# Attention, state-space and routed layers on one core: links of two VectorE chains placed apart

## The reference, cut to what matters

```python
def _L0_attn_a_ref(x, norm_w, Wq, bq, Wk, bk, Wv, bv, Wo, bo):
    ...
    scores = jnp.einsum('bhqd,bhkd->bhqk', q, k) * scale
    causal = jnp.triu(jnp.ones((T, T), dtype=bool), k=1)
    scores = jnp.where(causal, jnp.asarray(-jnp.inf, dtype=scores.dtype), scores)
    attn = jax.nn.softmax(scores, axis=-1)
    out = jnp.einsum('bhqk,bhkd->bhqd', attn, v)
    ...
# state-space layer, one step over the 512 tokens, for 16 states
    decay = jnp.exp(A[None] * dt[:, :, None])
    inp = dt[:, :, None] * xt_[:, :, None] * bt[:, None, :]
    h = decay * h + inp
    y = jnp.einsum('bdn,bn->bd', h, ct)
```

## Time and profile before

| | us |
|---|---|
| median of 3 runs | 2156.38 |
| lowest and highest | 2152.31, 2167.72 |
| the profiled execution | 2161.24 |
| its span, first to last instruction | 2159.4 |

### The profile page before, as it was taken

One profiled execution on the slowest core, in us unless ns is written; L12 is line 12 of the kernel. 1 busy time (PEld: TensorE's weight loads), 2 busy tenths in 40 slices (PEclk: granted clock), 3 DMA queues, 4 the chain that ended last, 5 costly groups with the idle time before them and its releaser, 6 DMA issues.

```text
span 2159.4 us, 33647 instructions
## 1 busy us (share of the span) xinstructions
PE 1842.8 (85%) x11409; PEld 1132.2 (52%) x11440; DVE 1684.1 (78%) x2586; ACT 1407.4 (65%) x2724; POOL 1040.1 (48%) x930
## 2 busy tenths in 40 slices
PE   5779888998989798988989898898989898877775
PEld 3446454645556464645556464655656464635333
DVE  5343678889788888879787888879887888987783
ACT  2445767686676767677675867677675767574531
POOL 0000364556555464646555464646555464666430
PEclk8999999999999999999999999999999999999998
DMA  4312377666767576667767686666767676652110
GB/s 115 83 52 59 93 152 153 145 142 150 159 140 159 124 170 140 151 128 154 158 148 157 129 171 130 146 142 149 156 141 157 133 157 135 139 112 61 45 59 10
DMA packets 185916, 275.53 MB, mean 128 GB/s; under 512 B 33537, under 2 KB 125586, under 8 KB 185746
## 3 DMA queue, kind: packets, MB, share of 16 engines
q1 hardware_dynamic: 155506, 163.27, 30.5%
q0 software_dynamic: 30240, 110.11, 27.6%
HBM read 128.58 MB, written 34.08 MB: 75 GB/s over the span
## 4 chain that ended last, share of the span: by engine, by line
PE 44%; ACT 19%; DMA 16%; SPq 7%; issue 6%; DVE 5%; POOL 2%; ACTq 0%; POOLq 0%; DVEq 0%
PE bank L314 7%; DMA sk<-qk_parts 7%; PE bank L518 5%; PE bank L323 5%; SPq L726 5%; ACT dec L910 3%; PE bank L372 3%; ACT pt L795 3%; PE bank L395 3%; PE bank L420 3%; PE bank L501 3%; DMA qk_parts<-parts 3%; DMA out<-X 3%; PE bank L482 3%; PE bank L308 2%
## 5 line engine op out<-in xcount | busy, mean ns | idle before, releaser
L1158 DVE TENSOR_TENSOR_SCAN hc<-dec,inp 128x1024 f32<-128x1024 f32 x256 | 613.1, 2395 | 33.0 <-ACT dec L910 28.6
L1331 POOL TENSOR_TENSOR inp<-u,b_all 128x512 f32<-128x512 f32 x256 | 341.1, 1332 | 421.9 <-DVE hc L1158 177.5
L795 ACT ACTIVATE pt<-bank 128x512 f32<-128x512 f32 x640 | 373.8, 597 | 220.4 <-PE bank L397 217.6
L372 PE MATMUL bank<-sk,sq 96*128 96x512 bf16 (+3 forms) x1024 | 279.6, 312 | 95.4 <-DMA sk<-qk_parts 64.4
L1337 POOL TENSOR_TENSOR inp<-u,b_all 128x512 f32<-128x512 f32 x240 | 350.0, 1458 | 18.8
L910 ACT ACTIVATE dec<-dt,a_neg 128x511 f32<-128x511 f32 x512 | 338.0, 717 | 31.4 <-DVE hc L1158 31.4
L1167 DVE TENSOR_TENSOR hc<-hc,bank 128x1024 f32<-128x1024 f32 x242 | 293.6, 1213 | 50.6 <-PE bank L557 49.9
L395 PE MATMUL bank<-sq,sk 98*128 98x512 bf16 (+3 forms) x1024 | 275.4, 307 | 34.1 <-ACT pt L795 28.1
L1344 POOL DMA_DIRECT2D y<-hc x210 | 185.6, 884 | 244.8 <-DMA y<-hc 122.9
L1026 DVE TENSOR_REDUCE mall<-bank 128x1 f32<-128x512 f32 x256 | 172.6, 674 | 100.3 <-PE bank L374 100.0
L372 PEld LDWEIGHTS bank<-sk,sq 96*128 96x128 bf16 x1024 | 102.3, 100 | 213.9 <-DMA sk<-qk_parts 73.0
(11 more groups left out here) (168 smaller groups left out, 3534.2 us busy)
## 6 DMA issues: line engine op xcount, KB each, us to landing
y<-hc POOLq DMA_DIRECT2D x210, 512.0 KB, 5.5
b_all<-b_kept SPq DMA_DIRECT2D x256, 256.0 KB, 4.0
qk_parts<-parts SPq DMA_DIRECT2D x96, 256.0 KB, 2.5
sq<-qk_parts SPq DMA_DIRECT2D x384, 64.0 KB, 3.6
sk<-qk_parts SPq DMA_DIRECT2D x384, 64.0 KB, 3.8
X<-in_x SPq DMA_DIRECT2D x16, 512.0 KB, 5.9
out<-X SPq DMA_DIRECT2D x16, 512.0 KB, 5.9
sq<-hlt SPq DMA_DIRECT2D x256, 2.0 KB
```

The lines of the kernel that those rows point to most:

```text
L372: mm(dst[:, o:o + n], sq[0:KS, slot, h, qb * P:(qb + 1) * P], sk[0:KS, slot, h, 0:n], start=True, stop=False)
L795: A(pt[:, n % PT, :], score_bank[unit % 2][:, :], ACT.Exp).then_inc(exp_done.sem, 1)
L1158: V.tensor_tensor_scan(h, d, v, 0.0, ALU.mult, ALU.add).then_inc(scan_done.sem, 1)
L1331: first = G.tensor_tensor(inp[:, n % 2, 0, :], u[:, 0, :], b_all[:, k % 3, :], ALU.mult)
```

## The change

The four operations of `finish_maxima` become functions of their own, and so do the two of `head_norm`, each signalling by a semaphore of its own in place of the shared `dve_own`. Their places: join behind the scan of p = 5; high part behind the maximum of p = 6, low part behind the product of p = 6; transpose behind the maximum of p = 7, where all four stood. Reciprocals at p = 4 as before; the multiplication at p = 5, behind the maximum there. What is computed is the same, and so is the number of operations. The other engines' orders don't change.

```diff
--- before.py
+++ after.py
@@ -112,7 +112,7 @@
               "gated": 246, "add_x3": (251, 251), "in1": 265, "out1": 268, "add_up1": (277, 280), "stats_q": -102}
     POOL_AT = {"rsqrt_f": 99, "rsqrt_s": 124, "rsqrt_q": -104, "inputs": 151, "rsqrt_l": 254, "low": (111, 266)}
     SP_AT = {"parts": (-43, -4), "load_x": -119, "store_b": 155, "store": 281}
-    FINISH = 14
+    JOIN_DVE = 5
     HEADS_PE, HEADS_DVE = 4, 4
 
     ctx = ExitStack()
@@ -259,12 +259,16 @@
         m_stacked = tally("max_rows_stacked", TB, 16)
         mx_ready = tally("scores_for_max", UN)
         mx_done = tally("maxima", UN)
+        joined = tally("blocks_joined", 1)
+        high_done = tally("high_parts_of_maxima", 1)
+        low_done = tally("low_parts_of_maxima", 1)
         negm_done = tally("negative_maxima", 1)
         st_ready = tally("scores_ready", UN)
         exp_done = tally("exps", UN)
         pv_done = tally("products_with_values", SETS)
         ot_done = tally("outputs_copied", 1)
         heads_turned = tally("outputs_turned", 1)
+        sums_done = tally("sums_of_exps", 1)
         heads_done = tally("outputs_normalised", 1)
 
         var = [tally(f"variance{k}", 1) for k in range(4)]
@@ -1028,27 +1032,37 @@
                     V.tensor_reduce(mall[:, w, h, 0:4], max_bank[m % 2][:, :].rearrange("p (k n) -> p k n", k=TB),
                                     AXX, ALU.max).then_inc(mx_done.sem, 1)
 
-            def finish_maxima(G):
-
-                w = G % 2
+            def join_blocks(G):
+
                 dve.wait_ge(mx_done.sem, mx_done.at(G))
-                V.tensor_reduce(mall[:, w, :, 5], mall[:, w, :, 0:3], AXX, ALU.max).then_inc(dve_own.sem, 1)
-                dve.wait_ge(dve_own.sem, dve_own.one())
-                four = mall[:, w, :, 3:7]
-                V.tensor_scalar(hl[:, 0, :, :], four, -1.0, None, ALU.mult).then_inc(dve_own.sem, 1)
-                dve.wait_ge(dve_own.sem, dve_own.one())
-                V.scalar_tensor_tensor(hl[:, 1, :, :], four, -1.0, hl[:, 0, :, :], ALU.mult,
-                                       ALU.subtract).then_inc(dve_own.sem, 1)
+                V.tensor_reduce(mall[:, G % 2, :, 5], mall[:, G % 2, :, 0:3], AXX, ALU.max).then_inc(joined.sem, 1)
+
+            def negate_high(G):
+
+                dve.wait_ge(joined.sem, joined.at(G))
+                V.tensor_scalar(hl[:, 0, :, :], mall[:, G % 2, :, 3:7], -1.0, None, ALU.mult).then_inc(high_done.sem, 1)
+
+            def negate_low(G):
+
+                dve.wait_ge(high_done.sem, high_done.at(G))
+                V.scalar_tensor_tensor(hl[:, 1, :, :], mall[:, G % 2, :, 3:7], -1.0, hl[:, 0, :, :], ALU.mult,
+                                       ALU.subtract).then_inc(low_done.sem, 1)
+
+            def turn_maxima(G):
+
                 dve.wait_ge(m_stacked.sem, m_stacked.at(G - 1))
-                dve.wait_ge(dve_own.sem, dve_own.one())
+                dve.wait_ge(low_done.sem, low_done.at(G))
                 V.transpose(hlt[:, :], hl[:, :, :, :].rearrange("p a h q -> p (a h q)")).then_inc(negm_done.sem, 1)
+
+            def head_sums(G):
+                dve.wait_ge(heads_turned.sem, heads_turned.at(G))
+                V.reciprocal(rc[:, :, :], pv_bank[:, :].rearrange("p (t h i) -> p t h i", t=TB, h=HG)[:, :, :, HD]
+                             ).then_inc(sums_done.sem, 1)
 
             def head_norm(G):
                 g = G % NG
-                dve.wait_ge(heads_turned.sem, heads_turned.at(G))
+                dve.wait_ge(sums_done.sem, sums_done.at(G))
                 pv = pv_bank[:, :].rearrange("p (t h i) -> p t h i", t=TB, h=HG)
-                V.reciprocal(rc[:, :, :], pv[:, :, :, HD]).then_inc(dve_own.sem, 1)
-                dve.wait_ge(dve_own.sem, dve_own.one())
                 V.tensor_tensor(ao[:, :, g * HG * HD:(g + 1) * HG * HD].rearrange("p t (h i) -> p t h i", h=HG),
                                 pv[:, :, :, 0:HD], rc[:, :, :, None].to_broadcast([P, TB, HG, HD]),
                                 ALU.mult).then_inc(heads_done.sem, 1)
@@ -1272,17 +1286,26 @@
                 for p in range(UN):
                     if 0 <= UN * q + p + LM < UN * NQ:
                         maximum(UN * q + p + LM)
-                    if FINISH == 2 * p and 0 <= q + 1 < NQ:
-                        finish_maxima(q + 1)
-                    if p == HEADS_DVE and 0 <= q - 1 < NQ:
-                        head_norm(q - 1)
+                    if 0 <= q + 1 < NQ:
+                        if p == JOIN_DVE + 1:
+                            negate_high(q + 1)
+                        if p == JOIN_DVE + 2:
+                            turn_maxima(q + 1)
+                    if 0 <= q - 1 < NQ:
+                        if p == HEADS_DVE:
+                            head_sums(q - 1)
+                        if p == HEADS_DVE + 1:
+                            head_norm(q - 1)
                     side_work(2 * (UN * q + p))
                     if p in STEP_AT:
                         scan(k + STEP_AT[p])
                     if p in PRODUCT_AT:
                         product(k + PRODUCT_AT[p])
-                    if FINISH == 2 * p + 1 and 0 <= q + 1 < NQ:
-                        finish_maxima(q + 1)
+                    if 0 <= q + 1 < NQ:
+                        if p == JOIN_DVE:
+                            join_blocks(q + 1)
+                        if p == JOIN_DVE + 1:
+                            negate_low(q + 1)
                     side_work(2 * (UN * q + p) + 1)
```

## The result

The changed kernel takes 2175.11 us in the median of 20 runs (2166.51 to 2185.88), the kernel before, run beside it, 2162.34 (2151.43 to 2178.14, 20 runs). The ratio is 1.0063, with a 95% interval of 1.0043 to 1.0082: the change makes the kernel slower by 0.6%, about 13 us. The forecast was 4 us slower; the direction is right and the time lies in the range, but the size was too small by a factor of three.

What follows compares the result with a forecast made beforehand. No engine was full; TensorE mostly led but was stopped by one DMA chain waiting, through SyncE's in-order queue, for VectorE's transpose. +6.1 - 2 gave about +4 us: median 2161 us, range 2142 to 2182.

Steps and rivals of the forecast that it cites:

- The stretch from reciprocal to transpose has no slack, and SyncE carries it to TensorE: At one place of the frame, a VectorE delay passes undiminished through transpose, SyncE and DMA to TensorE's stacked-keys wait.
- the 11 waits that the prediction counted: TensorE's waits for the stacked keys at the same place in 11 frames, from 0.42 to 3.13 us.
- Heads, +0.34: Reciprocal to scan of p = 5: the multiplication moved behind the maximum makes the scan 0.34 us later.
- Chain, 4.30 us from the scan's end to the transpose's end: Join to transpose in G = 34: holds behind POOL make it 4.30 us against 4.09, so +0.21 us.
- The rival in which `lg` keeps its lead: Chain in G = 34: low part not held, `lg` starts before POOL's second multiplication; 2148 us, chance 0.2.
- Together +0.55 us for a frame ... Times the 11 frames that show the wait: +6.1 us: Transpose +0.55 us later per frame, reaching SyncE and TensorE's wait at 1047.85; over 11 frames +6.1 us.
- The fill, -2 us: Before the scans begin, POOL is idle and a transpose 0.68 us earlier arrives whole at 3 to 4 waits: -2 us.
- The other places absorb: Elsewhere in the frame, VectorE's waits soon after each changed place swallow gains or losses of some tenths; taken as 0.
- I find no second: Claim that only one place of the frame passes a VectorE delay undiminished to TensorE.

Runs made afterwards that it cites:

- delay at G mod 4 = 2: Kernel before with 0.95 us of repeated joins ahead of the transpose, only in groups with G mod 4 = 2; ratio 1.0100.
- delay at G mod 4 = 0: Kernel before with 0.95 us of repeated joins ahead of the transpose, only in groups with G mod 4 = 0; ratio 0.9954.
- later load: Kernel before with SyncE issuing the load of the next x row two positions later, behind the stack's last third; ratio 0.9887, median 2137.00 us.
- heads apart: Kernel before with only the heads' multiplication moved behind the maximum of p = 5, chain of the maxima unchanged; ratio 1.0048.

## Why the prediction was right in direction and too small in size

1. *The stretch from reciprocal to transpose has no slack, and SyncE carries it to TensorE*: right. The delay at G mod 4 = 2 costs 1.0%, the one at G mod 4 = 0 nothing, and with slack in SyncE's queue most of the cost goes (to 0.3%, and to 0.1% for the change). Of the 11 waits that the prediction counted the shortest is 0.38 us, at 680.14, not 0.42.
2. *Heads, +0.34*: right. Scan 3.58 us behind the reciprocal (1023.74 against 1020.16), forecast 3.59, before 3.25.
3. *Chain, 4.30 us from the scan's end to the transpose's end*: 4.29 in this frame, high 0.20, low 0.41 (0.38 forecast), `lg` 1.23 (1.22 forecast). The rival in which `lg` keeps its lead was decided by a tenth of a microsecond: it came 0.07 behind POOL. In 4 of the 14 such groups from G = 10 on `lg` does last 0.18 (there the high part lasts 0.85 instead).
4. *"Together +0.55 us for a frame ... Times the 11 frames that show the wait: +6.1 us"*: this is the step that was mis-sized. The shift of T2 is right (10.15 against 9.62; in the mean 0.61). The term stands for what a later T2 costs, and that is more than itself, because TensorE then runs at half clock behind more of its waits: 1.6 us for each stretch at half clock, and one such stretch more or less behind K4 is three times the shift. I had taken a wait to cost its length. In the profiles the wait at K4 grew by 1.07 us and the stretch behind it by another 0.81; for the delay of 0.95 us it is 1.44 and 1.10. Of the wait's growth only the part by which T2 is later is shown to be the change's, as said under the table.
5. *The fill, -2 us*: the 13th group's reciprocal comes at 400.6 instead of 402.6 us, 2.0 earlier, and TensorE's waits for the `hlt` rows fell from 7.6 to 5.9 us in sum. Right in mechanism; that the size fits as well is partly luck, since the same reciprocal comes anywhere from 397.5 to 402.1 us in profiles in which the chain was not touched (later load, heads apart).
6. *The other places absorb*: right for the delay at G mod 4 = 0 (distance +1.0 and then -1.0). The wait before the second row's stack, at 1105.85 us in the profile before, even became shorter, 1.87 to 1.18 us in the mean, so that over the whole span TensorE's waits for `sk` grew only from 64.4 to 68.3 us (about 70 was forecast). This second place, with its wait in 11 of the 12 frames, is one that the prediction's "I find no second" passes over.
7. *The tail*, which the prediction left out: from the reciprocal of group 60 to the end 293.4 us before and 299.1 after. It has 52.1 and 65.7 us of half clock. One profile each, and 299.8 and 292.3 in others of these kernels: scatter for a good part, left open.

The medians' 13 us can be rebuilt in part, as an estimate. Eleven frames of 0.61 us are 6.7. The clock adds about half as much again (the 0.54 of the straight line), 3.6, and the fill takes 2 away: 8 us. The runs' own clocks speak for more: from clock and span, the changed kernel has 194 us at half clock in the mean of its 20 runs, and the kernel before 178 to 184 in its runs beside the experiments. In time that is at most 5 to 8 us in place of the 3.6, and a sum of at most 10 to 13. The measured interval is 9 to 18 us, so a few microseconds may have a cause that is not shown.

In the profiles 12 frames of 1.65, less 2.0, plus 5.7 give the 23.6 us by which the spans differ; the medians differ by 13, so in a usual pair of runs the same parts are about half as large. Why T2 to K4, which is DMA for the most part, is 0.1 to 0.4 us shorter in the profile of before than in the others with this queue (26.91 against 27.00 to 27.36) was not looked into; it may be that this one execution was lucky there, and then a part of the 1.07 us of wait is its luck.

## What to carry to other kernels

Placing the links of a dependent chain apart saves only some tenths of a microsecond for a group, and each link must be looked at in its new place: what GpSimd is running at that time, and which wait used to hide it. Follow the last link past its own consumer, into the in-order queue of whoever waits for it; here a transpose of 0.2 us stood, through SyncE, in front of a store, a load and a stack. And when the matrix engine's wait is the end of such a path, price an added microsecond of wait at more than one (here about 1.5), and look for slack in the queue before shortening the work: one number in a table of DMA places gave 1.1%, where the rearranged chains cost 0.6%.

## What the runs showed of the hardware that I had not expected

- Waits of TensorE of 1.92 and 2.90 us were followed by a stretch at 1.2 GHz, that of 1.92 us at a cost of 1.6 us on top; waits of 1.30 us and, in the changed kernel at 1057.21 us, of 1.95 us in the same place were not. In the kernel before a wait of 1.87 us was, one of 2.14 us was not: the length of the wait alone doesn't decide. Over the 12 frames the half-clock time behind K4 was 13.7 us before, 37.5 with the change, 47.8 with the delay and 0.0 with the later load.
- Independent VectorE operations of 0.14 to 0.20 us cost 0.06 (join) and 0.11 us (high) from start to start (1025.94, 1026.00; 1026.59, 1026.70), with fulfilled semaphore waits between them, against 0.19 to 0.28 in the chain of the earlier trace rows.
- The scan beside POOL's `hw` operation of 1.25 us became longer by that operation's whole length (3.56 instead of 2.28 us), although POOL's started 0.15 us behind it. In the seven such frames of that profile POOL's operation started 0.15 to 0.48 us behind the scan, and each time the scan ended 2.16 us behind the end of POOL's operation, about its own length alone. Once `hw` started 0.58 us behind the scan (1756.56): there the scan lasted 2.29 us, and `hw` 2.45 instead of 1.25.
